# Four chains in place of two in the written-out engine orders of a two-layer decoder

## What is computed

```python
x = LN(x + mamba(x))              # in-projection, conv of 4, silu, selective scan of 16 states, gate, out-projection
x = LN(x + xattn0(x, ctx))        # kv = ctx @ Wk.T + b; softmax(LN(x @ kv @ kv.T / 16) * g + b): 256 x 256
x = LN(x + moe0(x))               # 8 experts of 176 wide, top 2, and a shared one of 352
x = LN(x + hgrn(x))               # gated linear recurrence over the tokens, rms norm, out-projection
x = LN(x + (1-g)*x + g*A(ctx))    # A: sigmoid of a similarity, kept where it is among the top 76 of its row, symmetrised
x = LN(x + moe1(x))               # 8 experts of 128 wide, top 2, and a shared one of 256
```

## Time and profile before

| | us |
|---|---|
| runs of the kernel before: median of 3 (lowest, highest) | 618.33 (615.70, 619.99) |
| span of the profiled execution, first to last instruction | 616.0 |
| median above that span | 2.3 |
| TensorE busy in the span | 523.1 |
| VectorE busy in the span | 498.5 |
| mean granted TensorE clock, of full | 0.925 |

### The profile page before, as it was taken

The page is one execution under the profiler, slowest core; times in us unless marked ns, Lnnn a source line. Parts: engine busy times, 40 slices in busy tenths (PEclk is TensorE's granted clock), DMA queues, the critical chain, the costliest instruction groups (busy, mean ns, idle before and its releaser), DMA issues.

```text
span 616.0 us, 8787 instructions
## 1 busy us (share of the span) xinstructions
PE 523.1 (85%) x2416; PEld 372.7 (60%) x2416; DVE 498.5 (81%) x1133; ACT 428.5 (70%) x962; POOL 266.5 (43%) x418
## 2 busy tenths in 40 slices
PE   4956674898776899999889998899999899989856
PEld 3534453566653567767566677676776767767634
DVE  2089999998989999999986979999899996544332
ACT  2597579699968867897966986995798692332211
POOL 1088567346785522647432565564344421101110
PEclk9876587699979999999989999899999999999969
DMA  7295020382204460166005550560272047042000
GB/s 201 79 377 201 1 70 1 101 264 87 69 1 112 127 194 2 50 196 197 0 1 151 144 147 5 167 202 1 77 232 64 2 129 235 0 129 94 10 0 9
DMA packets 29823, 63.59 MB, mean 103 GB/s; under 512 B 4752, under 2 KB 8592, under 8 KB 29392
## 3 DMA queue, kind: packets, MB, share of 16 engines
q1 hardware_dynamic: 29776, 63.04, 33.3%
HBM read 61.91 MB, written 1.11 MB: 102 GB/s over the span
## 4 chain that ended last, share of the span: by engine, by line
PE 42%; DVE 26%; ACT 15%; issue 10%; POOL 3%; SPq 2%; DMA 1%; DVEq 0%; POOLq 0%; ACTq 0%
PE work L610 24%; PE work L667 9%; DVE acc L1187 5%; DVE st L1171 5%; ACT dA L962 5%; PE work L586 3%; PE h_bank L586 3%; DVE m L1136 2%; ACT L962 2%; DVE wk L1140 2%; ACT L831 2%; DVE h_tok L1089 2%; POOL dbu L548 2%; DVE du L1105 2%; DVE bst L1014 2%
## 5 line engine op out<-in xcount | busy, mean ns | idle before, releaser
L548 POOL TENSOR_TENSOR dbu<-du,b_rows 128x512 f32<-128x512 f32 x128 | 163.1, 1275 | 82.1 <-DVE st L1171 60.6
L962 ACT ACTIVATE dA<-dts,a_neg 128x127 f32<-128x127 f32 x512 | 156.9, 355 | 17.2 <-DVE st L1171 16.1
L1171 DVE TENSOR_TENSOR_SCAN st<-dA,dbu 128x512 f32<-128x512 f32 x128 | 155.1, 1214 | 6.4 <-ACT dA L962 6.1
L586 PE MATMUL h_bank<-ident,st 128*128 128x128 f32 x512 | 89.1, 305 | 41.2 <-DVE acc L1187 32.4
L610 PE MATMUL work<-stream,xsT 128*128 128x352 f32 (+1 forms) x320 | 111.1, 485 | 4.5 <-ACT xsT L831 1.9
L586 PEld LDWEIGHTS h_bank<-ident,st 128*128 128x128 f32 x512 | 66.3, 156 | 74.3 <-DVE st L1171 55.6
L1187 DVE SCALAR_TENSOR_TENSOR acc<-h_bank,c_cols,acc 128x512 f32<-128x512 f32 x128 | 92.9, 726 | 0.5 <-PE h_bank L586 0.4
L610 PEld LDWEIGHTS work<-stream,xsT 128*128 128x128 f32 x320 | 59.4, 200 | 33.8 <-issue 3.6
L493 POOL TENSOR_SCALAR var<-mv 128x1 f32<-128x1 f32 x56 | 12.7, 227 | 132.0 <-DVE mv L1015 131.1
L831 ACT ACTIVATE h_t<-work 128x384 f32<-128x384 f32 (+2 forms) x64 | 30.8, 482 | 37.6 <-PE work L586 37.5
L962 ACT ACT_TABLE_LOAD x43 | 55.2, 1283 | 0.8
(11 more groups left out here) (159 smaller groups left out, 824.4 us busy)
## 6 DMA issues: line engine op xcount, KB each, us to landing
stream<-in_stream SPq DMA_DIRECT2D x72, 352.0 KB, 3.5
stream<-in_stream SPq DMA_DIRECT2D x32, 384.0 KB, 3.7
b_rows<-b_dram SPq DMA_DIRECT2D x32, 256.0 KB, 4.4
stream<-in_stream SPq DMA_DIRECT2D x8, 360.0 KB, 3.7
stream<-in_stream SPq DMA_DIRECT2D x8, 256.0 KB, 2.7
wg<-in_wg SPq DMA_DIRECT2D x1, 1280.0 KB, 8.5
wu<-in_wu SPq DMA_DIRECT2D x1, 1280.0 KB, 11.0
wd<-in_wd SPq DMA_DIRECT2D x1, 1280.0 KB, 13.6
```

The costliest lines, as they stand in the source:

```text
L548: gp.tensor_tensor(tile, du[:, batch % 2, :, lo:hi], b_rows[:, b % 2, k:k + 1, :].to_broadcast([P, ET, P]), ALU.mult).then_inc(s["dbu_read ...
L586: return nc.tensor.transpose(dst, src, ident[:, :])
L962: last = A(dA[i % DA_RING][:, t, 1:P], dts[:, batch % 2, t, lo + 1:hi], ACT.Exp, scale=a_neg[:, t, k:k + 1])
L1171: V.tensor_tensor_scan(st[:, i % ST_RING].rearrange("p t l -> p (t l)"), dA[i % DA_RING].rearrange("p t l -> p (t l)"), dbu[:, i % DBU_RIN ...
```

## The change

The two chains `0` and `1` become four: `m` (out and xat0), `f` (ffn0), `h` (hgrn) and `g` (ffn1). A unit's `out` may now stand before the last steps of the unit before it in ffn0, and a unit's hgrn before the end of the unit before it in ffn1. For this each chain gets its own `r`, `xsT`, `bst`, `mv`, `var`, `rstd` and root counter; `row2` and `row5`, which carry rows from a mixer to its feed-forward, get two slots; every kind of row has its own semaphore; the router of ffn0 has its own `nmx`, `es`, `ri`. A few waits guard the slots (before `xat0` 4, `hgrn` 6 and 7, the last `D`s, and `adj` 14). SBUF for it comes from `STREAM_RING` 6 to 5, `ACC_RING` 4 to 3, and shared `i8`, `if8`, `wa`, `wb`. SyncE gets an order string of its own, with chains for loads, stores, `b_rows` spreads and stream chunks. All strings in `ORDER` and `BANK` are new. What an engine computes in a step is the same as before.

```diff
-ACC_RING = 4
+ACC_RING = 3
-STREAM_RING = 6
+STREAM_RING = 5
...
-    layer0 = [("out", k) for k in range(6)] + [("xat0", k) for k in range(5)] + [("ffn0", k) for k in F0.steps]
-    layer1 = [("hgrn", k) for k in range(8)] + [("ffn1", k) for k in F1.steps]
+    mixer0 = [("out", k) for k in range(6)] + [("xat0", k) for k in range(5)]
...
-        "0": [(stage, u, k) for u in range(U) for stage, k in layer0],
-        "1": [(stage, u, k) for u in range(U) for stage, k in layer1],
+        "m": [(stage, u, k) for u in range(U) for stage, k in mixer0],
+        "f": [("ffn0", u, k) for u in range(U) for k in F0.steps],
+        "h": [("hgrn", u, k) for u in range(U) for k in range(8)],
+        "g": [("ffn1", u, k) for u in range(U) for k in F1.steps],
+        "l": [("load", part, 0) for part in range(7)],
+        "b": [("store", b, 0) for b in range(B)],
+        "r": [("spread", u, 0) for u in range(U)],
+        "c": [("chunk", i, 0) for i in range(U * 3 * F0.chunks)],
...
 ORDER = {
     "pe": [
-        "ppp0ppppss00pppassssssaaaaaaaaaaaaasssssssssssss0ssp00sss00000spppssspsppsssss0000ss0ss0000s000000s0000s0s00s0",
...
-        "1110000001011110011111111111111111111111111111111111",
+        "pppppppppmsssssmssssssassssssasssmmmssssppssmmmspspppspsmmmmssfsfsfffsfsfffffsffssfffppsspmmmfssfffsfsfsfmssaa",
...
+        "ffgfggghhhhhhgggghhggggggggggggggggggggggppsmmmfhhhg",
...
+    "sp": [
+        "llllcllccbrcrlbcrccccccxccccbcrccccwcccccccccrccccccbccrcccccoccwcwccccwcccccocrccccrccccccccccccccccccocwccc",
+        "cccccoccwccccccccccccocccccccccccccoccccccoo",
...
-        r = [sb(f"r{i}", [P, H]) for i in range(2)]
-        xsT = [sb(f"xsT{i}", [P, HT, P]) for i in range(2)]
+        r = [sb(f"r{i}", [P, H]) for i in range(4)]
+        xsT = [sb(f"xsT{i}", [P, HT, P]) for i in range(4)]
...
                 if stage == "xat0" and k == 4:
+                    if b >= 2:
+                        dve.wait_ge(*read("ffn0", b - 2))
                     normalize(("xat0", 3), 2, b)
```

More of the change, by code:

```diff
@@ L102 @@
     ],
     "dve": [
[L104 to L107, removed]
@@ L168, in banks, with part_of @@
     return first + BANKS.get((stage, k), [])
-ROOTS0 = [("out", 4), ("xat0", 1), ("xat0", 3), ("ffn0", F0.sum)]
-ROOTS1 = [("hgrn", 4), ("hgrn", 5), ("hgrn", 6), ("ffn1", F1.sum)]
+MIX0, FFN0, MIX1, FFN1 = range(4)
+ROOTS = [[("out", 4), ("xat0", 1), ("xat0", 3)], [("ffn0", F0.sum)],
+         [("hgrn", 4), ("hgrn", 5), ("hgrn", 6)], [("ffn1", F1.sum)]]
+def part_of(stage):
+    return {"out": MIX0, "xat0": MIX0, "ffn0": FFN0, "hgrn": MIX1, "ffn1": FFN1}[stage]
 def decoder(nc, d, b_dram, out):
-    pe_order, dve_order, act_order, pool_order = (timeline(engine) for engine in ("pe", "dve", "act", "pool"))
+    pe_order, dve_order, act_order, pool_order, sp_order = (
+        timeline(engine) for engine in ("pe", "dve", "act", "pool", "sp"))
     with ExitStack() as ctx:
@@ L295, in decoder @@
         t8 = [sb(f"t8{i}", [P, 8]) for i in range(2)]
-        i8 = [sb(f"i8{i}", [P, 8], U32) for i in range(2)]
-        if8 = [sb(f"if8{i}", [P, 2]) for i in range(2)]
+        i8 = sb("i8", [P, 8], U32)
+        if8 = sb("if8", [P, 2])
         pr = sb("pr", [P, 3])
@@ L300, in decoder @@
         rest = sb("rest", [P, F0.experts])
-        wa = [sb(f"wa{i}", [P, 8]) for i in range(2)]
-        wb = [sb(f"wb{i}", [P, 8]) for i in range(2)]
+        wa = sb("wa", [P, 8])
+        wb = sb("wb", [P, 8])
         wf = [sb(f"wf{i}", [P, 8]) for i in range(2)]
@@ L317, in decoder @@
         b_stored = [sem(f"b_stored{i}") for i in range(2)]
+        x_loaded = [sem(f"x_loaded{i}") for i in range(2)]
         stream_loaded = [sem(f"stream_loaded{i}") for i in range(STREAM_RING)]
@@ L341, in root @@
         def root(stage, k, u):
-            roots = ROOTS0 if (stage, k) in ROOTS0 else ROOTS1
-            return rstd_ready[int(roots is ROOTS1)], len(roots) * u + roots.index((stage, k)) + 1
+            part = part_of(stage)
+            return rstd_ready[part], len(ROOTS[part]) * u + ROOTS[part].index((stage, k)) + 1
         def gated(n, u):
@@ L438, in load_chunk @@
             def load_chunk(i):
-                if i >= len(numbers):
-                    return
                 if i >= STREAM_RING:
@@ L481, in _ @@
-            store_rows(U - 1)
+            for stage, i, k in sp_order:
+                if stage == "load":
+                    load_part(i)
+                if stage == "store":
+                    store_b(i)
+                if stage == "spread":
+                    spread_b(i)
+                if stage == "chunk":
+                    load_chunk(i)
+                if stage == "xT":
+                    sp.wait_ge(*full("gate", LT * (i - 2) - 1))
+                    sp.dma_start(xT[:, i % 3], d["xT"][:, :, i * L:(i + 1) * L]).then_inc(s["xT_loaded"], 16)
+                if stage == "x":
+                    sp.wait_ge(*row(1, i - 2))
+                    sp.dma_start(x_rows[:, i % 2], d["x"][:, i, :]).then_inc(x_loaded[i % 2], 16)
+                if stage == "rows":
+                    store_rows(i)
@@ L1070, in ffn @@
                 elif k == f.sum:
-                    add_bank(f.stage, u, rows(rows_in, u), lay)
+                    if u:
+                        dve.wait_ge(*row(rows_in + 1, u - 1))
+                    add_bank(f.stage, u, rows(rows_in, u), (FFN0, FFN1)[lay])
                 elif k == "norm":
@@ L1200, in _ @@
                     if b:
-                        dve.wait_ge(*row(3, b - 1))
-                    add_bank("mamba", b, rows(0, b))
+                        dve.wait_ge(*row(2, b - 1))
+                    add_bank("mamba", b, rows(0, b), MIX0)
                 if stage == "out" and k == 5:
```

231 lines of the change are left out of this document (110 added, 121 removed).

## The result

The kernel after takes 573.8 us (median of 4 runs, 573.0 to 574.8) against 617.0 of the kernel before beside it: ratio 0.930, 95% interval 0.926 to 0.933. The change took 43 us off. I had forecast 599 us, 19.2 off by my sum, and the result lies outside my range.

A forecast was written before the change was run, and what follows sets the result against it. VectorE was taken to bound from 50 to 225 us, TensorE from 500 to 575, neither leading between; 7.8 + 2.0 + 9.4 = 19.2 us off a 616.0 span gave 596.8, with 2.3 to the median 599 us, range 579 to 619.

The forecast's parts named there:

- Table loads: ScalarE's table loads: 99 fall to 70, and by their share of the chain 7.8 us go, bounds 0 to 16.
- rival B: Whole kernel: loads were hidden, head a wash, only the tail gained and new waits take most; 615 us, chance 0.19.
- Head: Start of the kernel: earlier scan projection and second sequence's conv before the first scan near 38 us; 2.0 us gained.
- Tail: Last unit's hgrn: ffn1 steps of unit 6 fill TensorE's two waits and avoid its slow clock; 9.4 us, bounds 5 to 11.
- Four chains in the middle: Mixer and ffn0 steps filling each other's waits: taken as 0 beyond the table loads, bounds -8 to +15.
- Rival A: Middle: four chains close most of the 15.4 us of idle time left; 584 us, chance 0.25.
- About 8 us less idle from 225 to 500: Sign to look for: about 8 us of TensorE's idle time gone from 225 to 500, not 17 or 0.
- Ring 5, acc ring 3, added waits, SyncE's order: Smaller rings, new guards and SyncE's string: each taken as 0, ring 5 up to 3 us if chunks land late.
- rival C: Weight stream: five slots starve TensorE and the kernel is slower, 623 at 7 us landings; anything above 622 had chance 0.11.

The follow-up runs named there:

- e4: Kernel before with every silu computed as tanh, leaving 11 table loads: 614.7 us against 613.8, ratio 1.000.
- e5: Kernel after with the first 50 us ordered on TensorE, ScalarE and VectorE as in the kernel before: 578.2 us, ratio 0.935 to before.
- e1: Kernel after with the last unit's hgrn again behind all of unit 6's ffn1 on every engine: 586.2 us, ratio 0.954 to before.
- e18: Kernel after's code and rings, with the order of before up to 480 us and the new order for the rest: 604.0 us, ratio 0.978 to before.
- e17: Kernel after's code and rings, with the order of before up to 225 us and the new order for the rest: 589.8 us, ratio 0.958 to before.
- e8: Kernel before with only the two ring sizes of after (stream 5, acc 3), no order changed: 616.6 us against 618.8, ratio 0.998.
- e6: Kernel before with GpSimd's dbu products cut to 16 of 128 columns: 613.7 us against 618.8, ratio 0.992.
- e7: Kernel after with GpSimd's dbu products cut to 16 of 128 columns: 572.4 us, ratio 0.926 to before.

## Why the prediction was wrong

*Table loads, 7.8 forecast: 0 in the kernel before.* I took a share of the chain for a share of the time. e4 removed 88 loads for nothing. The likely reason, not shown, is that the chain of the earlier trace rows names one engine at each step, and with the load gone a neighbour that was nearly as late takes its place. My own remark that ScalarE idles 30% belonged here, not in rival B. Rival B was right in this half alone.

*Head, 2.0: 3.1 to 4.4 (e5).* Right in its mechanism, mis-sized: I had the first scan 2.4 us later, and it was 1.5 (36.70, 38.25). The 4.8 of conv less 1.5 is 3.3.

*Tail, 9.4: about 11.* The medians give 12.4 undone (e1) and 13.9 done alone (e18), but behind the last common step the traces give 10.8 and 11.4. The gaps were as read, 8.0, and the slow matmuls behind them cost 2.5 and not 1.5. I chose 9.4 under a bound of 11; the mechanism was right.

*Four chains in the middle, taken as 0: this is the step that failed.* e18 to e17 gives 14.2, and the stretch before 225 gives 16.0, of which the head is 4.4: 26 us in all, beyond even the bound of 15. Two errors. First, the bound. I counted idle time of the engine that bounds and held its busy time fixed, since no step's work changed. But busy time isn't work: VectorE lost 18.6 us of it, some 17 by standing still less often beside GpSimd (22.3 to 5.6), and TensorE 16.5, about half of them by the clock (the last section has the rows). Time that an engine spends slowed can be won as well. Second, the choice of 0. The largest sum of one engine's work up to a step and the other's from it is a floor; I read it as if the kernel sat on it. Rival A had the argument (many waits of a microsecond are what a second chain fills) and I set it aside because VectorE was full. VectorE was full, but in part with standing still. TensorE's idle time in the three middle stretches fell by 16.1 us, from 34.9 to 18.8, close to the 15.4 that A had. A comes nearest in its mechanism; its 584 is 10 us too high, since it too counted idle time alone. "About 8 us less idle from 225 to 500" came out as 9.1 between steps (8.3 + 10.0 to 6.8 + 2.4). That it came near is luck: I had meant the table loads, and they had nothing to do with it.

*Ring 5, acc ring 3, added waits, SyncE's order, 0: right.* e8 measures the rings, and e18's first 480 us the rings with the own buffers and the added waits. Landings stay at 3.5 us in the median, no wait for `stream` appears, and rival C has nothing left.

*The sum.* 19.2 forecast, less 7.8 for loads that gave nothing, 1 to 2 more at the head, some 2 more in the tail, 26 in the middle: some 41, of 43.2 measured. The early part of the 26 is what was left over between e17 and the kernel after, so this sum is a check of size only.

Open: whether an order with two chains could reach the 26. The splices show that the gain is the order's, and where. That its TensorE string runs a mixer's steps ahead of the last ffn0 step of the unit before, in all seven places, is plain from the string; that it must, and so that the gain needs four chains, was only tried by searches that were too weak. Also open is how much of the clock's part is a cause and how much a result: TensorE waited less and its granted clock was higher, and no run holds one and moves the other.

## What to carry to other kernels

A share of the chain of waits is no price: before a term is taken from it, ask what is next late, and where an engine idles 30%, take 0 until something says otherwise. In two coupled engines at 81 and 85%, bound a new order's gain not by idle time alone but by idle time plus what clock and contention add to busy time (here some 8.5 us of TensorE's and 17 of VectorE's, though e6 and e7 put the worth of the 17 at 2 to 4). Cut two traces at the same steps, not at the same times; see at each cut what the other engine has still to do; and splice orders in time to place a gain. An early lead that was bought with another engine's put-off work lasts only if the later order has room for it.

## What was not expected of the hardware

VectorE stands still beside GpSimd, and only some of its instructions do. All 48 of one form in the trace of before (least, median and greatest ns):
```profile
L1021 DVE TENSOR_SCALAR row<-r,mv,rstd x48: 380/413/1501, 83.9 to 613.3; 128x256 f32<-128x256 f32 x48
```
15 of them overlap a `dbu` in time, with a mean of 890 ns, the other 33 have 418. Of the 15, 12 began behind the `dbu` and ended some 0.15 us behind its end; two began 0.16 and 0.22 us ahead of it and kept their time (389 and 421 ns), and those two `dbu` took 1347 and 1316 ns in place of some 1270. The Trainium skill, "SBUF — State Buffer", section "Who interferes with whom", says that whichever starts first gets the shared port pair for its whole instruction. The trace agrees with these 14. The one left began 0.08 us ahead and stood still all the same, 1501 ns.

The scans aren't touched: `st<-dA,dbu` takes 1211 ns in the mean of 66 that overlap a `dbu` and 1217 ns in 62 that don't. Of its two inputs only `dbu` lies in SBUF; `dA` is a PSUM bank. The stretched ones either read SBUF twice or copy within SBUF.

TensorE's 16.5 us less of busy time for the same matmuls are over a third of the 44.9, and not all of them are clock. The granted clock is at 0.78 of full in the first 140 us, 0.92 in the next 81, and 0.94 in the last 97, where 1.00 is 2.4 GHz; those are the stretches in which TensorE waited most. After, the last three are at 1.00. Added up over each span, the clock is at its lower level, half of full, for 92.8 us before and 65.2 after, and TensorE is busy for 64.3 and 47.2 us of these. The `wg` group of e1 takes 3.76 us there against 1.96, nearly twice; taken as twice, the clock gives an estimated (64.3 - 47.2) / 2 = 8.5 of the 16.5. Most of the rest is in how busy time is counted. A matmul of 256 columns stands in the trace with 0.38 us, yet 16 in a row take 3.62 us (at 524.53 after), 0.22 each; so each unbroken row of matmuls counts some 0.16 us that the next would have covered. There are 98 such rows before and 58 after: an estimated 6.5 us.
